# Graph convolution with residual norm: the one-hot comparison reads the loaded rows instead of labels that GpSimd makes

## The reference

```python
w = silu(edge_scalars @ Wfc1 / 4) @ Wfc2 / 8            # weights of each edge
e0, e1 = f0[edge_src], f1[edge_src]                      # gathered source features
mid0, mid1, mid2, mid3 = ...                             # w times e0, e1 and sh
cnt = clip(segment_sum(1, edge_dst), 1)
scal, vec = segment_sum(mid, edge_dst) / cnt             # mean over a node's edges
conv = alpha(scal) * concat(scal @ Wl2_s, vec @ Wl2_v)
x = layernorm(x + sc(x) + conv)
```

## Time and profile before

| | before |
|---|---|
| median of three runs | 993.56 us |
| the profiled execution | 993.99 us |
| its span | 992.3 us |
| busy: TensorE / weight loads / VectorE / ScalarE / GpSimd | 914.4 / 807.7 / 846.8 / 672.7 / 727.3 us |
| moved by DMA | 186.31 MB |
| granted TensorE clock, mean | 0.977 of full speed |

### The profile page before, as it was taken

The page is one execution under the profiler, slowest core; times in us unless marked ns, Lnnn a source line. Parts: engine busy times, 40 slices in busy tenths (PEclk is TensorE's granted clock), DMA queues, the critical chain, the costliest instruction groups (busy, mean ns, idle before and its releaser), DMA issues.

```text
span 992.3 us, 26855 instructions
## 1 busy us (share of the span) xinstructions
PE 914.4 (92%) x7944; PEld 807.7 (81%) x7944; DVE 846.8 (85%) x2587; ACT 672.7 (68%) x2061; POOL 727.3 (73%) x809
## 2 busy tenths in 40 slices
PE   2576999999999999999999989999999999999993
PEld 1465888888888888888888878898888888888883
DVE  2485888888888888888888968998999999999994
ACT  1232555555555555555555536998999999999997
POOL 6474767777776767776767317989988889998893
PEclk9787999999999999999999999999999999999997
DMA  4455444444444444444444337999999999999992
GB/s 149 156 90 176 135 134 125 136 126 133 136 124 134 133 127 138 122 136 129 130 137 126 101 110 210 282 285 291 291 285 289 287 289 307 291 285 293 290 284 106
DMA packets 86794, 186.31 MB, mean 188 GB/s; under 512 B 17438, under 2 KB 47930, under 8 KB 86651
## 3 DMA queue, kind: packets, MB, share of 16 engines
q1 hardware_dynamic: 67707, 148.78, 49.3%
q0 software_dynamic: 18944, 35.81, 14.4%
HBM read 119.58 MB, written 64.95 MB: 186 GB/s over the span
## 4 chain that ended last, share of the span: by engine, by line
PE 71%; issue 13%; POOL 10%; DVE 2%; ACT 2%; DMA 1%; SPq 0%; POOLq 0%; ACTq 0%; DVEq 0%
PE ps L682 12%; PE ps L742 9%; PE ps L646 9%; PE ps L664 9%; PE ps L680 8%; PE ps L651 6%; PE ps L752 5%; POOL xa L587 4%; PE ps L633 4%; PE ps L631 4%; PE ps L731 3%; POOL xa L583 2%; PE ps L625 2%; POOL gat L546 1%; POOL lab L595 1%
## 5 line engine op out<-in xcount | busy, mean ns | idle before, releaser
L546 POOL DMA_INDIRECT gat<-turned,srcs x196 | 187.8, 958 | 98.2 <-issue 82.5
L546 POOL DMA_INDIRECT gat<-spread,srcs x196 | 185.9, 948 | 63.4 <-issue 61.3
L802 ACT ACTIVATE e_sb<-ps 128x512 f32<-128x512 f32 x196 | 106.5, 594 | 152.0 <-PE ps L651 146.6
L742 PE MATMUL ps<-win,hot 60*128 60x162 f32 x2352 | 191.9, 309 | 1.7 <-ACT agg L834 0.2
L742 PEld LDWEIGHTS ps<-win,hot 60*128 60x128 f32 x2352 | 168.1, 188 | 19.0 <-issue 10.9
L682 PE MATMUL ps<-wy,mid 128*128 128x161 f32 x784 | 182.6, 315 | 0.0
L843 ACT ACTIVATE fin<-res,shift,rstd 128x160 f32<-128x160 f32 x392 | 172.1, 511 | 12.6 <-DVE shift L1138 11.0
L939 DVE SCALAR_TENSOR_TENSOR msg<-ps,sha,z 128x161 f32<-128x161 f32 x392 | 151.0, 385 | 13.9
L606 POOL TENSOR_TENSOR res<-agg,pre 128x640 f32<-128x640 f32 x98 | 151.5, 1546 | 9.7 <-ACT agg L834 7.8
L1130 DVE TENSOR_TENSOR hot<-column,lab 128x768 f32<-128x768 f32 x98 | 143.4, 1464 | 4.3 <-issue 2.4
L680 PE MATMUL ps<-wy,mid 128*128 128x97 f32 x784 | 141.8, 263 | 0.2 <-DVE mid L915 0.2
(11 more groups left out here) (97 smaller groups left out, 1614.2 us busy)
## 6 DMA issues: line engine op xcount, KB each, us to landing
win<-rows SPq DMA_DIRECT2D x392, 114.6 KB, 4.7
rows<-msg SPq DMA_DIRECT2D x98, 326.0 KB
xin<-x_g SPq DMA_DIRECT2D x98, 322.0 KB, 6.2
out<-fin SPq DMA_DIRECT2D x49, 640.0 KB, 7.0
gat<-turned,srcs POOLq DMA_INDIRECT x196
gat<-spread,srcs POOLq DMA_INDIRECT x196, 2.6
eas<-ea_t SPq DMA_DIRECT2D x5, 512.0 KB, 8.8
shs<-sh_t SPq DMA_DIRECT2D x1, 752.0 KB, 4.1
```

Source lines behind the costliest of these rows:

```text
L546: pool.indirect_dma_start(out=gat[:, slot, first:first + of.shape[1]], out_offset=None, in_=of, in_offset=bass.IndirectOffsetOnAxis(ap=src ...
L742: last = nc.tensor.matmul(agg_ps[b1][:, 2 * h + k, 0:SW], hot[side(h), b1, k, c, :], win[side(h), (b - 1) % RING, k, c, 0:SW], start=c == ...
```

## The change

The messages carry the number of the destination node modulo 512 (CYCLE, four tiles of 128), which is a bitwise AND on the integer table once, ahead of the edge stage. Tile k of a group then always compares with the numbers 128k to 128k+127, whichever group it is. A table `columns` of 2 x 128 numbers holds them for two tiles on partitions 0 to 63 and for the other two on partitions 64 to 127. VectorE compares `columns` directly with the label column of the loaded window. GpSimd's `lab` and the tables `tile_base` and `column` go, and the wait for the window's DMA moves from GpSimd to VectorE. Since numbers repeat every 512 nodes, the flag `general` is now also set if some four consecutive tiles have fewer than 180 edges (`spans`, `shortest`). The general path reads its node numbers from another tensor, and it isn't run with these inputs.

```diff
-        column = sb("column", [P, P])
+        columns = sb("columns", [P, 2, P])
-        tile_base = sb("tile_base", [P, NT // 2])
...
-                    pool.wait_ge(win_in[b], 16 * GROUP * (i + 1))
-                    if group_has(i, b, 2):
-                        pool.wait_ge(hot_ready, groups(i, b, 2))
-                    nc.gpsimd.tensor_tensor(
-                        lab[:, b0], win[:, b, :, :, LABEL],
-                        tile_base[:, bass.ds((RING * i + b) * 2, 2)].unsqueeze(2)
-                        .broadcast_to([P, 2, WC_ROWS]), ALU.subtract).then_inc(lab_ready, 1)
...
+            nc.vector.tensor_scalar(dsts_i[:], dsts_i[:], CYCLE - 1, None, ALU.bitwise_and
+                                    ).then_inc(dsts_low_ready, 1)
+            dve.wait_ge(dsts_low_ready, 1)
             nc.vector.tensor_copy(dsts[:], dsts_i[:]).then_inc(dsts_ready, 1)
...
+                nc.vector.tensor_tensor(spans[:], start_row[:, GROUP:NT + 1],
+                                        start_row[:, 0:NT + 1 - GROUP],
+                                        ALU.subtract).then_inc(spans_ready, 1)
...
+                nc.vector.tensor_reduce(shortest[:], spans[:], AX_X, ALU.min
+                                        ).then_inc(shortest_ready, 1)
...
+                nc.vector.scalar_tensor_tensor(out=general[:], in0=shortest[:],
+                                               scalar=float(WINDOW), in1=general[:],
+                                               op0=ALU.is_lt, op1=ALU.add
+                                               ).then_inc(cycle_ready, 1)
...
-                    dve.wait_ge(lab_ready, groups(i, b))
+                    dve.wait_ge(win_in[b], 16 * GROUP * (i + 1))
                     if group_has(i, b, 2):
                         dve.wait_ge(agg_done, groups(i, b, 2))
                     nc.vector.tensor_tensor(
-                        hot[:, b0].rearrange("p k c e -> p (k c) e"),
-                        column[:].unsqueeze(1).broadcast_to([P, 2 * WC_ROWS, P]),
-                        lab[:, b0].rearrange("p k c -> p (k c)").unsqueeze(2)
-                        .broadcast_to([P, 2 * WC_ROWS, P]), ALU.is_equal).then_inc(hot_ready, 1)
+                        hot[:, b0],
+                        columns[:].unsqueeze(2).broadcast_to([P, 2, WC_ROWS, P]),
+                        win[:, b, :, :, LABEL].unsqueeze(3).broadcast_to([P, 2, WC_ROWS, P]),
+                        ALU.is_equal).then_inc(hot_ready, 1)
```

More of the change, by code:

```diff
@@ L41 @@
 GROUP = 4
+CYCLE = GROUP * P
 RING = 4
@@ L147, in gnn_kernel @@
         widths = sb("widths", [1, NT])
+        spans = sb("spans", [1, NT - GROUP + 1])
         widest = sb("widest", [1, 1])
+        shortest = sb("shortest", [1, 1])
         general = sb("general", [1, 1])
@@ L156, in gnn_kernel @@
         g_dst = sb("g_dst", [P, P], I32)
+        g_node_i = sb("g_node_i", [P, 1], I32)
+        g_node = sb("g_node", [P, 1])
         g_same = sb("g_same", [P, P])
@@ L178, in gnn_kernel @@
         xa = sb("xa", [P, 2, GROUP + 1, P])
-        lab = sb("lab", [P, 2, 2, WC_ROWS])
         hot = sb("hot", [P, 2, 2, WC_ROWS, P])
@@ L237, in gnn_kernel @@
         pads_out = sem("pads_out")
+        dsts_low_ready = sem("dsts_low_ready")
         dsts_ready = sem("dsts_ready")
@@ L257, in gnn_kernel @@
         widest_ready = sem("widest_ready")
+        spans_ready = sem("spans_ready")
+        shortest_ready = sem("shortest_ready")
+        cycle_ready = sem("cycle_ready")
         over_ready = sem("over_ready")
@@ L284, in gnn_kernel @@
         g_spare_ready = sem("g_spare_ready")
+        g_node_ready = sem("g_node_ready")
+        g_low_ready = sem("g_low_ready")
         g_same_ready = sem("g_same_ready")
@@ L453, in load_tile @@
                                  ).then_inc(g_loaded, 16)
+                    with nc.allow_non_contiguous_dma("a number of each row, in the general path"):
+                        sp.dma_start(g_node_i[:], dst_rows[bass.ds(t * P, P)].unsqueeze(1)
+                                     ).then_inc(g_loaded, 16)
                 load_tile(0)
@@ L510, in more_constants @@
                 for ap, pattern, base, mult in (
-                        (column[:], [[1, P]], 0, 0),
-                        (tile_base[:], [[GROUP * P, NG], [P, 2]], 0, 0),
+                        (columns[:].rearrange("p k e -> p (k e)"), [[1, 2 * P]], 0, 0),
                         (bound[:], [[P * P, CH]], 0, P),
@@ L518, in more_constants @@
                                    channel_multiplier=mult).then_inc(iotas_set, 1)
+                pool.wait_ge(iotas_set, 5)
+                nc.gpsimd.iota(columns[HALF:P].rearrange("p k e -> p (k e)").bitcast(I32),
+                               pattern=[[1, 2 * P]], base=2 * P,
+                               channel_multiplier=0).then_inc(iotas_set, 1)
                 pool.wait_ge(iotas_set, 6)
[L520 to L523, removed]
                 nc.gpsimd.memset(pads[:], 0.0).then_inc(pads_set, 1)
@@ L961, in prepare_order @@
                                         ALU.is_gt).then_inc(greater_ready, 1)
-                dve.wait_ge(iotas_set, 7)
-                for ap in (column, tile_base, bound, node_base, g_label, g_spare):
+                dve.wait_ge(iotas_set, 6)
+                for ap in (columns, bound, node_base, g_spare):
                     nc.vector.tensor_copy(ap[:], ap[:].bitcast(I32)).then_inc(iotas_ready, 1)
+                nc.vector.tensor_scalar(g_label[:].bitcast(I32), g_label[:].bitcast(I32),
+                                        CYCLE - 1, None, ALU.bitwise_and
+                                        ).then_inc(g_low_ready, 1)
+                dve.wait_ge(g_low_ready, 1)
+                nc.vector.tensor_copy(g_label[:], g_label[:].bitcast(I32)).then_inc(iotas_ready, 1)
                 dve.wait_ge(greater_ready, 1)
@@ L975, in prepare_tiles @@
                 nc.vector.tensor_copy(wrong_sum[:], wrong_ps).then_inc(heads_out, 1)
-                dve.wait_ge(iotas_ready, 6)
+                dve.wait_ge(iotas_ready, 5)
                 dve.wait_ge(heads_out, 2)
@@ L1017, in prepare_flag @@
                                         ).then_inc(widest_ready, 1)
+                dve.wait_ge(spans_ready, 1)
+                nc.vector.tensor_reduce(shortest[:], spans[:], AX_X, ALU.min
+                                        ).then_inc(shortest_ready, 1)
                 dve.wait_ge(widest_ready, 1)
@@ L1048, in _ @@
                 with dve.Fori(0, T) as t:
-                    dve.wait_ge(g_loaded, 32 * t + 32)
-                    nc.vector.tensor_scalar(g_same[:], g_dst[:], g_msg[:, LABEL:AW], None,
+                    dve.wait_ge(g_loaded, 48 * t + 48)
+                    nc.vector.tensor_copy(g_node[:], g_node_i[:]).then_inc(g_node_ready, 1)
+                    dve.wait_ge(g_node_ready, t + 1)
+                    nc.vector.tensor_scalar(g_same[:], g_dst[:], g_node[:], None,
                                             ALU.is_equal).then_inc(g_same_ready, 1)
-                    nc.vector.tensor_tensor(g_moved[:], g_spare[:], g_msg[:, LABEL:AW],
+                    nc.vector.tensor_tensor(g_moved[:], g_spare[:], g_node[:],
                                             ALU.subtract).then_inc(g_spare_ready, 1)
@@ L1067, in _ @@
                     dve.wait_ge(g_offset_ready, t + 1)
-                    nc.vector.tensor_tensor(g_row[:], g_moved[:], g_msg[:, LABEL:AW], ALU.add
+                    nc.vector.tensor_tensor(g_row[:], g_moved[:], g_node[:], ALU.add
                                             ).then_inc(g_row_ready, 1)
@@ L1141, in step @@
                     ).then_inc(shift_ready, 1)
+            dve.wait_ge(pads_ready, 1)
             node_steps(dve, step)
```

3 lines of the change are left out of this document (2 added, 1 removed).

## The result

The changed kernel takes 1036.92 us (median of four runs, 1033.17 to 1038.62) against 994.59 us for the kernel before beside it. The ratio is 1.042, with a 95% interval of 1.039 to 1.046. **It is slower by 42 us, where 6.5 us of gain were forecast.** The profiled execution took 1038.62 us, its span is 1036.9 us.

What follows compares the result with a forecast made beforehand. DMA was taken to set nearly the whole node-stage pace. Gains of 2.7 (early stalls), 3.0 (window landing to use) and 0.8 us (DMA idle at 830 to 840), set-up 0, made 6.5: 993.99 to 987.5 us, range 980 to 993.

Steps and rivals of the forecast that it cites:

- The stall of before: Node stage: GpSimd's window wait ahead of `res` and `xa` reached TensorE's transposes 11 times, for 12.4 us.
- R1: Rival, node stage: DMA is only kept busy by queued requests, not the bound; 982 or 977 us, chance 0.25.
- Step 1: Removing GpSimd's `lab`, 98 instructions at 521 ns mostly spent held: nothing counted for the instruction itself.
- Step 4: VectorE's `hot` reads `win` instead of `lab`: cost 0, at most 0.05 us a group; it keeps meeting `xa` through the port lock.
- Step 2: Window wait moves to VectorE ahead of `hot`, with `shift`, `cnt` and `pre` queued behind; deadline some 2.2 us later.
- step 5: Set-up: AND and cast taken as 0, at most 0.4 us; edge-stage additions about 0.8 us if not covered.
- my 1 us: Sign that the set-up is right: the first aggregation begins within 1 us of 591.4.
- R3: Rival, slower: waits at VectorE's `hot` stall more than those at `lab` did; 999 to 1017 us, chance 0.07.
- R4: Rival, slower: `hot` itself grows by reading the window, 1062 us at twice the time per number; chance 0.03.
- R2: Rival, node stage: throughput fixed and nothing won at the ends; gain 0 to 3 us, 991 to 994, chance 0.17.
- the slower end of the forecast: Case with half the early gain and the set-up paid: gain of 3.55 us, 990.4 us.
- Step 3 (a): Before 660 us, idle DMA engines get work earlier as TensorE's transposes no longer wait for `xa`: 2.7 us gain.

Runs made afterwards that it cites:

- `lab` kept: Changed kernel with GpSimd again waiting for the window and computing a lab-like result nobody reads, VectorE still reading the window: 993.33 us against 994.11.
- the spacer: Changed kernel plus an unread 128x6 GpSimd subtraction on constants between `xa` and `res`, without a window wait: 989.39 us against 994.11.
- shift-first kernel: Changed kernel with `shift` placed ahead of `hot` in VectorE's order: 985.95 us against 994.11, and 987.46 against 994.09 when measured again.
- memset kernel: Changed kernel plus an unread 128x6 GpSimd memset, which reads nothing, between `xa` and `res`: 1040.67 us against 994.09.

## Why the prediction was wrong

**The stall of before: right.** With the wait for windows in GpSimd's queue (`lab` kept) the time is 993.3 us, with the spacer and no wait 989.4: the wait costs 3.9 us. The shift-first kernel, which differs in the order too, stands 6 to 7 us below `lab` kept. The forecast sum was 6.5.

**That DMA sets the pace is not shown.** The prediction's 3.89 us divides the bytes of a stretch by the rate at which the same stretch moved them, so it must give back the pace of 3.91, whatever the bound is. And a DMA share of 1.0 turned out to be no sign of a ceiling. From 660 to 960 us, with `res` in four pieces and with the spacer:

```profile
660.00:960.00 300.00, 291.11 (x2912) 253.59 (x2909) 294.69 (x896) 276.63 (x821) 300.00 (x448) 1.00 1.00 283
660.00:960.00 300.00, 292.15 (x3020) 263.01 (x3017) 282.15 (x931) 286.76 (x853) 289.56 (x311) 1.00 1.01 296
```

The first has GpSimd busy for 300 of 300 us and a share of 1.00 at 283 GB/s, the second a share of 1.01 at 296. This is what R1 said of the share, kept busy by requests that queue. Two of R1's signs stand in the spacer and the shift-first kernels: 296 GB/s, and hardly a wait for windows. The forecast's sign, `hot` idling for `win` for 5 to 15 us, is absent (0.6 us). The steps of `res` there are 3.88 and 3.83 us on average. DMA still reaches the engines at the stores: `fin` waits for one 10 times (7.2 us) and 23 times (12.6 us). What sets the pace of these two kernels stays open.

**Step 1 is the step that failed.** The steps from 660 to 960 us are 4.48 us on average, beyond the 3.95 that the prediction named as its sign of being wrong. Step 1 counted "nothing for the instruction itself", since GpSimd's own work was not the bound. I had the row in hand: `lab` at 0.91 us beside `hot`, held. I read it as idle time that costs nothing, and did not ask what the held instruction was in turn keeping back, and what `res` would meet once it stood some 0.1 us earlier. The term put at nothing is the one that decides: in the steady state `res` gets ahead of `shift` in every other step, `shift` takes 1.5 us and not 0.15, and this is worth +1.1 us for two groups, 45 us in all. With a held instruction put back in its place (the spacer) the time is 989.4 us.

**Step 4 named the very lock and used it for the wrong pair.** I asked only how `hot` and `xa` meet. The rule of the Trainium skill, "SBUF — State Buffer", section on two separate sides, for a VectorE instruction with two SBUF inputs, covers `shift` too, whose four numbers I took for too small to matter. The traces agree with it: the subtraction is held beside `hot` (0.91 us), the memset is not (0.10), the form of `shift` with one tensor input is not (0.56 for four), and an instruction of 0.15 us takes 1.5 us behind one that began 0.04 us ahead. With the rule applied to every neighbour in the two queues, `res` would have been a rival with a price.

**Step 2 was right on the wait**: `hot` waits for no window. Its list of what is queued behind, `shift` first and `fin` behind that, was the list of the victims, of a delay from another side.

**Step 4 on reading win, and step 5: right** (with `lab` kept, 0.999; `hot` at 1366 ns). The first aggregation begins at 592.62 us, 1.3 later than before and so outside my 1 us, in an execution in which VectorE's first instruction, behind a DMA in both, began at 8.67 us and not at 6.70. What the 1.3 us are due to was not tested. **Rivals:** R3 and R4 ended on the slower side, and both of their mechanisms were absent. R2 and R1 don't describe the changed kernel either. In the sum for the slower end of the forecast, 6.5 - 1.35 - 1.2 - 0.4, the last 0.4 is explained nowhere: the set-up's 0.4 is already in the 1.2. Without it that end is 990.0, which changes nothing here. The range reached 993 and the time is 44 us above it, because no case held a new collision between GpSimd and VectorE.

**Step 3 (a)** can be seen at first: the second aggregation begins at 597.24 and the ten steps after it are 3.72 us, where the kernel before had stalls. In these steps, too, `lab` is gone, and `res` still begins 0.06 us or more behind `shift`. So taking `lab` out makes the loss possible but doesn't start it. The first held `shift` is at 649.77 us:

```profile
641.84 0.15 DVE L1162 SCALAR_TENSOR_TENSOR shift<-stats,rstd 128x4 f32<-128x4 f32 x1
641.92 1.55 POOL L608 TENSOR_TENSOR res<-agg,pre 128x640 f32<-128x640 f32 x1 [0.82 <-ACT agg L836]
642.34 1.76 ACT L845 ACTIVATE fin<-res,shift,rstd 128x160 f32<-128x160 f32 x4 [0.49 <-DMA out<-fin]
...
649.73 1.54 POOL L608 TENSOR_TENSOR res<-agg,pre 128x640 f32<-128x640 f32 x1 [0.69 <-ACT agg L836]
649.77 1.51 DVE L1162 SCALAR_TENSOR_TENSOR shift<-stats,rstd 128x4 f32<-128x4 f32 x1
```

What tips the engines into the pair of 5.27 and 3.71 us steps stays open. Two steps before, `fin` waits 0.49 us for a store's DMA; in the memset kernel it waits 0.42 us for one at 625.72 us, and two steps later, at 633.16, `shift` is held for the first time. With the spacer `fin` waits so 10 times from 660 to 960 us, and `shift` is never held: where a held instruction keeps `res` back, such a wait does no harm. No run took the wait away. By their times the other runs of the change fell into the pair too.

## What to carry to other kernels

An instruction that is held up for most of its time may be holding back what follows it. Before taking one away on VectorE or GpSimd, write down for each neighbour in both queues what it reads, and ask which pair now starts within a tenth of a microsecond of each other. If a tiny operation lies on the chain and a large GpSimd operation can get ahead of it, try the tiny one at a place where its successor would have waited for the other engine anyway. Here that was ahead of `hot` (986.0 and 987.5 us).

A group whose mean is 835 ns where four numbers per partition are computed is the thing to look for in a profile: a held instruction counts as busy, and the view of waits shows only its victims.

## What the runs showed of the hardware

- A 128x4 operation of VectorE with two tensors from SBUF took 1.51 us when a 128x640 addition of GpSimd had begun 0.04 us earlier, and 0.15 us when it came first. The same product with one tensor and a number per partition, as four operations of which three began inside that addition, took 0.56 us for the four.
- A 128x6 subtraction of GpSimd beside VectorE's `hot` took 0.91 us, and 0.19 us without `hot` beside it; a 128x6 memset beside `hot` took 0.10 us.
- A lead of 0.04 us of `res` over `shift` went with a stable alternation of steps of 5.27 and 3.71 us that lasted for 41 pairs.
- The DMA engines' share was 1.00 to 1.01 at 283 GB/s in one kernel and at 296 GB/s in another, so a full share didn't mean the highest rate.
- A semaphore from VectorE to GpSimd put `res` 0.38 us behind the start of `shift`; the held spacer put it 0.09 us behind.
